# A graph-attention kernel: VectorE's score scans and ScalarE's exponentials moved ahead of the second of three sub-batches

## What is computed

```python
aij = dt @ (w2_W.T @ a_vec) + jnp.dot(a_vec, w2_b)      # dt = feat[dst] - feat[src]
ss = h_src @ w2_W.T + w2_b
m = jax.ops.segment_max(aij, dst, num_segments=n)
aexp = jnp.exp(aij - m[dst])
denom = jax.ops.segment_sum(aexp, dst, num_segments=n)
alpha = aexp / denom[dst]
res = jax.ops.segment_sum(alpha[:, None] * ss, dst, num_segments=n)
```

## Time and profile before

| | us |
|---|---|
| median of 3 runs (12,473.06 to 12,480.08) | 12,474.11 |
| the profiled execution | 12,483.0 |
| its span, first to last instruction | 12,481.2 |
| from the first gather of the stage (346.75) to the end of its last | 4,316 |

### The profile page before, as it was taken

How to read it: one execution, slowest core, us unless ns; L and a number is a source line. 1 busy time by engine, 2 the same in 40 slices (tenths; PEclk the granted TensorE clock), 3 DMA queues, 4 the chain that set the end, 5 groups by cost and what they waited for, 6 DMA issues and landing times. The chain is left out here.

```text
span 12481.2 us, 259020 instructions
## 1 busy us (share of the span) xinstructions
PE 7914.2 (63%) x99382; PEld 6537.2 (52%) x99382; DVE 7676.7 (62%) x11973; ACT 4861.3 (39%) x7540; POOL 7790.6 (62%) x7325
## 2 busy tenths in 40 slices
PE   2566666666666664999994444444444443699999
PEld 2455555555555554999992111111111111699999
DVE  4677777777777775878783333233323333687878
ACT  1455555555555553666660000000000000466666
POOL 6677777777777773323267777777777777231323
PEclk7555555555555556999997777777777776799999
DMA  5233333333333334999993222222222222699998
GB/s 100 83 102 99 102 96 102 98 100 103 99 100 99 103 94 175 371 354 364 352 355 68 64 66 66 66 64 65 66 66 64 65 66 52 248 352 343 354 348 321
DMA packets 942150, 1951.42 MB, mean 156 GB/s; under 512 B 316829, under 2 KB 539891, under 8 KB 941675
## 3 DMA queue, kind: packets, MB, share of 16 engines
q1 hardware_dynamic: 562633, 1661.09, 36.1%
q0 software_dynamic: 235776, 185.47, 9.9%
q10 hardware_dynamic: 143650, 103.69, 3.0%
HBM read 1571.49 MB, written 381.38 MB: 156 GB/s over the span
## 5 line engine op out<-in xcount | busy, mean ns | idle before, releaser
L666 POOL DMA_INDIRECT attend_and_count_rows<-table,attend_and_count_ring x3136 | 3308.9, 1055 | 1078.0 <-issue 1005.4
L1570 POOL DMA_INDIRECT judge_edges_src_rows<-table,judge_edges_ring x3136 | 2978.5, 950 | 955.7 <-issue 943.2
L709 PE MATMUL attend_and_count_counts<-attend_and_count_hot_hi,attend_and_count_hot_lo 128*128 128x98 bf16 x15680 | 1466.6, 279 | 1554.9 <-DVE attend_and_count_hot_lo L740 854.2
L1456 POOL DMA_INDIRECT x_sb<-slot_sums,last_slot x588 | 951.7, 1618 | 2400.7 <-DMA slot_sums<-propagate_norm_whole 1213.8
L709 PEld LDWEIGHTS attend_and_count_counts<-attend_and_count_hot_hi,attend_and_count_hot_lo 128*128 128x128 bf16 x15680 | 1238.8, 137 | 1785.1 <-DVE attend_and_count_hot_lo L740 915.7
L1643 PE MATMUL judge_edges_p_hid<-judge_edges_attr_feat,judge_edges_w 128*128 128x512 f32 x784 | 614.3, 876 | 2155.9 <-DVE judge_edges_src_feat L1686 2155.9
L822 ACT CAST attend_and_count_stage<-attend_and_count_counts 128x784 uint8<-128x784 f32 x1960 | 1494.2, 813 | 453.6 <-PE attend_and_count_counts L709 448.3
L740 DVE TENSOR_TENSOR attend_and_count_hot_hi<-ramp_hi,attend_and_count_key_hi 128x784 bf16<-128x784 bf16 x1960 | 976.8, 560 | 985.7 <-ACT attend_and_count_key_lo L791 984.1
L1643 PEld LDWEIGHTS judge_edges_p_hid<-judge_edges_attr_feat,judge_edges_w 128*128 128x128 f32 x784 | 192.7, 276 | 2456.1 <-issue 2456.1
L1686 DVE STREAM_TRANSPOSE judge_edges_src_feat<-judge_edges_src_rows 128x512 f32<-128x512 f32 x196 | 203.1, 1036 | 2052.3 <-DMA judge_edges_src_rows<-table,judge_edges_ring 2052.3
L740 DVE TENSOR_TENSOR attend_and_count_hot_lo<-ramp_lo,attend_and_count_key_lo 128x1024 bf16<-128x1024 bf16 x1960 | 1234.1, 692 | 0.0
(11 more groups left out here) (282 smaller groups left out, 14129.3 us busy)
## 6 DMA issues: line engine op xcount, KB each, us to landing
propagate_mean_raw<-matrix SPq DMA_DIRECT2D x372, 1568.0 KB, 8.8
propagate_norm_raw<-matrix SPq DMA_DIRECT2D x372, 1568.0 KB, 8.9
matrix<-attend_and_count_stage SPq DMA_DIRECT2D x245, 784.0 KB, 5.2
scan<-attend_and_count_out SPq DMA_DIRECT2D x196, 272.0 KB
inject<-attend_and_count_zeros SPq DMA_DIRECT2D x49, 1024.0 KB, 4.6
attend_and_count_rows<-table,attend_and_count_ring POOLq DMA_INDIRECT x3136
judge_edges_src_rows<-table,judge_edges_ring POOLq DMA_INDIRECT x3136, 3.3
judge_edges_dst_rows<-inject SPq DMA_DIRECT2D x195, 256.0 KB
```

Source lines behind the costliest of these rows:

```text
L666: nc.gpsimd.indirect_dma_start(out=rows[:, u, g, j, :], out_offset=None, in_=D.table0[:, :], in_offset=rows_of(ring[:, u, g, j:j + 1])).th ...
L709: last = nc.tensor.matmul(counts[:, r % 2, k // 4, NH * (k % 4):NH * (k % 4) + NH], hot_lo[:, u, slot, :], hot_hi[:, u, slot, :], start=Tr ...
L1456: nc.gpsimd.indirect_dma_start(out=S.x[:, h, :], out_offset=None, in_=D.slot_sums[0:j * BLOCK, :], in_offset=rows_of(S.last_slot[:, h:h + ...
L1570: nc.gpsimd.indirect_dma_start(out=src_rows[:, u, lane, :], out_offset=None, in_=D.table2[:, :], in_offset=rows_of(ring[:, u, lane:lane + ...
```

## The change

In steps with three sub-batches `scan_scores` (VectorE) and `weigh` (ScalarE) stand behind m0 instead of behind m1. Steps with two sub-batches keep their order. No instruction is added or removed, and GpSimd's, TensorE's and SyncE's programs are the same. The load of the flags and `pack_rows` stay where they were, between m1 and m2.

```diff
@@ dve
             def one(i, t, is_last):
-                for m in SHARE[t][:-1]:
+                compare(i, SHARE[t][0])
+                scan_scores(i, t)
+                for m in SHARE[t][1:]:
                     compare(i, m)
-                scan_scores(i, t)
-                compare(i, SHARE[t][-1])
                 scan_sums(i, t)
@@ act
             def one(i, t, is_last):
-                for m in SHARE[t][:-1]:
+                keep_counts(i, SHARE[t][0])
+                weigh(i, t)
+                for m in SHARE[t][1:-1]:
                     keep_counts(i, m)
-                weigh(i, t)
                 if not is_last:
                     load_flags(*after(i, t))
                     pack_rows(*after(i, t))
```

## The result

The changed kernel takes 12,377.3 us (median of 6 runs, 12,376.0 to 12,388.6) against 12,482.3 us for the kernel before (6 runs, 12,473.1 to 12,493.4). The ratio is 0.9913, 95% interval 0.9903 to 0.9924: faster by 105 us. I had forecast 12,500 us, a little slower, and a range from 12,400.

What follows compares the result with a forecast made beforehand. Issuing 3,136 GpSimd gathers was taken to bound the stage. Lockouts +57, the twelve mid-compare gathers -15, short losses -13 and tail -3 us gave +26 on the 12,474.1 us median: 12,500 us, 8-in-10 range 12,400 to 12,600.

Steps and rivals of the forecast that it cites:

- Where m2 meets the gathers: Step placing the third sub-batch's moved compare against gathers: 39 lockouts from fourth steps, about 10 from second, 49 in all.
- lockout: Gather of 4.42 to 4.46 us held beside a step's first compare; 30 before, some 3.0 us each, 49 forecast.
- case B: First gather 0.98 to 1.25 us after a compare's start, a later one at 4.32; said to lead to a lockout.
- Case C: First gather 0.00 to 0.51 us after a compare's start, a later one at 3.12; said to lead to a lockout.
- case A: First gather 0.52 to 0.97 us after a compare's start, a later one at 3.72; next step's gather at 0.16, free.
- Second steps: Third sub-batch's compare 4.70 us behind the second's, gather at 0.91, case A, free; lockouts in about 10 turns only.
- the twelve of the middle: Twelve gathers of 1.7 to 3.6 us, in mid-compare of the third sub-batch after GpSimd pauses; their going saves 15 us.
- short loss: Gather lengthened beside a compare: 0.2 to 0.8 us each, mean 0.45, about 221 us in all.
- The term of 13 us for short losses of m2: Loss at the third sub-batch's compare in second steps falls from 0.63 to 0.31 us: -13 us over 49 turns.
- The 3 us at the tail: Stage's end behind its last gather: third sub-batch's compare and sums come 2.9 us earlier, -3 us.
- The frame: Issuing gathers bounds the stage: 3,308.9 us busy plus 1,005.4 us issue; compute engines follow with some 15 us of slack.
- Lockouts go away: Rival: in fourth steps case B turns into case A, fewer lockouts remain; 12,413 us at 20, 12,383 at 10; chance 0.22.

Runs made afterwards that it cites:

- h3: Changed kernel with ScalarE copying the next step's keys ahead of the packing in a turn's fourth step; ratio 1.0007 to the kernel before.
- h4: Kernel before with an extra, unused 128x224 VectorE multiply directly ahead of the third sub-batch's compare; ratio 0.9985 to the kernel before.
- f1: Kernel before with VectorE waiting for its own numerator scan, ahead of the next step's first compare; ratio 0.9934 to the kernel before.
- f4: Changed kernel with each compare in 16 instructions of half the length instead of 8; ratio 1.0618 to the kernel before.
- f2: Kernel before with VectorE waiting for the end of its last compare ahead of the sums; ratio 0.9944 to the kernel before.
- e4: Changed kernel with only ScalarE's new order kept, VectorE's order undone; ratio 0.9948 to the kernel before.
- g3: The same kernel as h3, run on a chip where the kernel before took 15,110 us; ratio 0.9963 to the kernel before.

## Why the prediction was wrong

**The step that failed** is in "Where m2 meets the gathers", the fourth step: "All lead to a lockout. Not so where the pack waits for its rows and the next compare no longer follows the sums directly (about 7 of 49 turns)". The exception became the rule, and its size was read from no row of a fourth step: before the change the run was broken behind 7 second steps and behind no fourth one. m2 fell as I said: 41 times in case B and 6 in C. But the next compare came 0.28 to 0.67 us behind the sums (the middle half), and of the 39 lockouts expected there 4 came, all where the compare did follow directly. Two things that I held apart act together. ScalarE reaches the packing 1.05 us sooner, as written, and found its rows landed in the earlier trace rows. Yet how far the chain runs behind the gathers isn't fixed. Before, packing of the next turn's first step started 2.7 us after its last gather's end (median), now 2.2, with rows as the wait in 189 steps of 196. From m1 it starts 10.7 us instead of 9.55. That moves the keys, copied behind it, from 10.7 to 11.9 us behind m1, while the sums end 3.0 us sooner, at 11.9 instead of 14.9. So a compare whose keys had been there 3.8 us ahead of it now starts 0.5 us late (medians). h3, in which the keys come ahead of the packing, shows by its 38 lockouts that this wait was the step the prediction lacked. I had the durations for this sum in the earlier trace rows and took the packing's place from before.

**Case C leads to a lockout:** wrong, and not read from a row. Before the change m2 never fell in C; I had the gather's start in the next compare and took the rest from B. h4 shows 55 of C without one.

**The condition for a lockout** itself, "when that compare follows the sums of a three-sub-batch step without a pause", was right as far as it went, and f1 shows it by an added wait. What I missed is the second half, an instruction lengthened in m2, which the start times stood in for: before the change, m2 in case A had its eighth instruction lengthened 58 times of 61 where the run was unbroken, and in case B never.

**Second steps:** right, and this is most of the gain. m2 came 4.69 us behind m1 (4.70), 38 of 47 in case A, the next compare's gather at 0.13, free. That took away the 21 lockouts of before. The other steps, in which I expected about 10, had none either: in 9 of the 47 m2 was in case C.

**The terms.** With 4 lockouts in place of 49 the prediction's own sum gives 26 x -3.0 - 31 = -109 us, and 105 were measured. Each term by itself fits less well. 26 lockouts fewer, and the twelve of the middle gone, took 109.3 us out, of which the twelve are 18.5 (I had 15) and a lockout 3.5 (I had 3.0, net of a short loss that would come back). The term of 13 us for short losses of m2 measured 0.5 over the whole stage; that gathers no longer held now have short losses of their own, an estimated 26 x 0.45 = 12 us by the prediction's mean, would account for it, but is not shown. The 3 us at the tail didn't show: the rest of the span is 8,167 us against 8,165. That score scan and exponentials cost nothing where they stand now held: VectorE still idles 5.40 us ahead of the m0 shown.

**The frame** held in every run of the table: the stage takes the gathers' busy time and 1,003 to 1,032 us. It was in the number of lockouts alone that I went wrong. The rival "Lockouts go away" had 0.22. It came nearest, but by another mechanism (m2 at 4.60 us behind m1 in fourth steps, hence case A), so that is luck. My range went down to 16 lockouts only, and so ended above the result.

The Trainium skill (SBUF — State Buffer, section "SBUF: two separate sides") has the port pair held for one instruction; for a VectorE instruction with two inputs in SBUF it says so only against a GpSimd operation that reads SBUF, a condition that the prediction left out. For the short losses the traces agree: a gather waits for the end of the compare instruction under way, and halving the instructions halved these losses (225 to 105 us). The lockouts don't fit, with 4.4 us through eight instructions and 8.9 us in f4, there through two compares in a row.

## What to carry to other kernels

Where one engine's issue bounds a stage, sum what its instructions take beyond their median, and sort the long ones by what the other engines did, back to their last pause: a neighbour that never pauses can hold an instruction for several of its own. A short wait for its own last result on an engine with time to spare may be the cheapest edit, here 0.7% by one line; with the shorter instructions of f4, pauses of over 3 us were not enough. And when a change brings an engine that follows the bound closer to it, work out anew everything that starts when the bound's results land, since slack shown in the trace of before belongs to the order of before. Count by place, too: the total of lockouts hid that the change acted by one cause in second steps and by another in fourth steps.

## What the runs showed of the hardware

- A gather that waits beside one of VectorE's compares ends 0.82 us after the end of a compare instruction. Mostly that is the instruction under way. But with eight instructions in a compare, after VectorE had run without a pause from the start of the compare before (7.3 us or more) and no instruction there was 0.04 us longer, the gather was held until the last of the eight had ended, 146 times of 148. Why a lengthened instruction prevents that, the traces don't show. That a pause of 0.21 us does for compares that follow sums, f1 and f2 show.
- A pause isn't enough everywhere. With 16 shorter instructions in a compare 265 gathers were held, against 4 with 8, and 241 of them sat in a compare begun after a pause, up to 8.9 us. In the table's kernels two gathers (e4, 1.8 and 2.0 us) were held in a compare that began after one.
- The kernel before took 15,110 us on one chip and 12,480 to 12,520 us on the others. In g3, profiled on the slow one, the median gather was the same 944 ns, but packing started 37 us after the last gather of its rows (median), against 2.3 us in the kernel before on the first chip.
